# Softmax denominators from added key tiles, and expert tiles in reverse order with fewer waits between scatter-adds, in a hybrid conv, attention and mixture-of-experts layer

## The chip, the cores and the metric

The kernel runs on 1 core of one Trainium2 chip. The metric is the device time of one execution in microseconds (us); the time before is a median of 3 runs. Engines are called TensorE (PE, and PEld for its weight loads), VectorE (DVE), ScalarE (ACT), GpSimd (POOL) and SyncE (SP, which issues DMAs).

## The reference

The input x is 8 batches of 512 channels on 16 x 16 positions, so 256 tokens of 512 channels each. Three residual layers follow each other:

```python
x = x + _L0_conv_ref(_gn(x), cfc_w, bn_w, bn_b)     # a gate per channel from mean, max, std
t = _to_tokens(x)                                   # [8, 256, 512]
t = t + _L1_attn_ref(_ln_t(t), w_q, w_k, w_v, w_o)
t = t + _L1_ffn_ref(_ln_t(t), ...)
```

The attention has 16 heads of 32. Scores go through 30 * tanh(s / 30), a causal mask (the window of 256 covers all keys) and a softmax; heads are joined by w_o. The feed-forward part adds a shared expert (width 512) and a mixture of 8 experts (width 256): each of the 2048 tokens goes to its two best experts, and their outputs are added with normalised weights.

## The kernel before

Everything is fp32; large products are split into high and low parts (three products each). The engines run one instruction stream each and meet at semaphores; the order on each engine is written out by hand, and an engine that waits holds up all that stands behind it on that engine.

**Attention.** One batch is one `step`; TensorE's step interleaves the scores and values of batch b with the projections of b+1 and the gate of b-1. The 16 heads form 4 groups of 4 (c or g from 0 to 3). The keys are 2 tiles of 128. For each pair of heads `probs` holds 2 x 384 columns: 256 queries for the first key tile, and queries 128 to 255 for the second. Scores (`group_scores`, L1486) go to ScalarE (`tanhs` L656, `exps` L663; tanh of group g waits for `pv_done` of group g-2), then GpSimd zeroes what the causal mask forbids (`mask`, L496), then TensorE's `head_values` (L1501) multiplies with v, and once more with a matrix of ones, which gives the softmax denominators on 32 partitions per head. Four heads lie side by side in the array and in the bank. In the ones products the first key tile takes 256 columns and the second 128 per head. VectorE inverts the denominators (`normalise`, L1072, L1075), ScalarE and GpSimd split the result into high and low (`att_high` L668, `att_low` L502). GpSimd also takes the power for the layer norms (`rstd_of`, L487); VectorE's `second_norm` (L1042) waits for it, TensorE's `gate_transposes` (L1456) for the norm. VectorE's `affine` (L1021), the copies of Q and K out of the bank (L1067) and of the gate's partial products (`partial_out`, L1083) come in that order; TensorE's `gate_logits` (L1533) wait for the last.

**Shared expert and routing.** Eight batches of `shared` on TensorE. Meanwhile VectorE works out the routing: how many 128-row tiles each expert gets, the slot of each token (`pair_slots`, L1263 to L1273), the expert of each tile (`tile_experts`, L1277 to L1281), and one-hot matrices (`one_hots`), which TensorE multiplies into token numbers, weights and destination rows of each slot (`place`, L1669; `slots_out`). GpSimd and ScalarE split the expert weights (`weight_low` L548, `weight_high` L741). SP stores each batch's tokens with the shared part to the output, and 128 filler rows behind it.

**Routed experts.** NTILES = 39 tiles of 128 slots, by expert. Per tile: GpSimd gathers 128 token rows (`gather`, L570), TensorE transposes them, multiplies with the expert's weights (L1406), transposes (L1711) and multiplies again (L1720); VectorE scales by the slot's weight into one of three buffers `yo` (`expert_out`, L1377), and GpSimd adds the rows to the output with an accumulating indirect DMA (`scatter_add`, L580). Two tiles of one expert have no token in common; tiles of different experts may. Slots without a token go to the filler rows. Each scatter-add waits until the one before has landed (`y_added`).

## Time and profile before

| what | value |
|---|---|
| median of 3 runs | 744.7 us (744.04 to 745.97) |
| the profiled execution | 744.78 us, span 743.1 us |
| granted TensorE clock, mean | 0.988 |
| PE busy | 646.3 us (87%) |
| PEld busy | 523.6 us (70%) |
| DVE busy | 402.7 us (54%) |
| POOL busy | 277.6 us (37%) |
| ACT busy | 262.0 us (35%) |
| chain that ended last | PE 57%, DMA 26%, DVE 10%, issue 4%, ACT 2%, POOL 1% |
| of it, scatter-adds of `yo` | 25% |

Shares are of the span. Busy times overlap between engines. A matmul's record lasts until its modelled end, and the next begins before that, so the distance between starts tells more than the duration. The chain is followed back from the last instruction, at each step to what released it.

### The profile page before, as it was taken

To read this page: it belongs to the slowest core of one execution; us is meant where nothing else is said; L and a number is where in the kernel's file an instruction comes from. 1 tells how busy PE (TensorE), PEld (TensorE's weight loads), DVE (VectorE), ACT (ScalarE), POOL (GpSimd) and SP (SyncE) were. 2 spreads that over 40 slices of the span, in tenths; PEclk is the share of its full clock that TensorE was granted. 3 is DMA by queue.
4 is the path that set the end of the run, shared out by engine and by line. 5 is a ranking of instruction groups with operands and counts; after the bars stand their busy time and mean duration, and the time that the engine had idled before them with its cause. 6 is when DMAs were issued, how large, how long until landed. Compare 5 with 4: busy or idle time off the path is not lost.

```text
span 743.1 us, 13600 instructions
## 1 busy us (share of the span) xinstructions
PE 646.3 (87%) x4859; PEld 523.6 (70%) x4860; DVE 402.7 (54%) x1021; ACT 262.0 (35%) x463; POOL 277.6 (37%) x324
## 2 busy tenths in 40 slices
PE   0112699999999999999999999999799999999991
PEld 0101688888888888888689899998566767667660
DVE  7886346566666656564556994223444443444430
ACT  7440155454454545364433223435112122121110
POOL 1980022323323222231411115857245445455431
PEclk9999999999999999999999999999999999999996
DMA  9540000010000101020125333442665555655533
GB/s 310 171 142 0 1 1 2 20 40 28 28 28 28 42 15 56 0 76 12 42 100 223 119 104 115 144 149 86 239 112 92 109 98 99 111 95 105 104 55 40
DMA packets 24786, 62.08 MB, mean 84 GB/s; under 512 B 3056, under 2 KB 7152, under 8 KB 23728
## 3 DMA queue, kind: packets, MB, share of 16 engines
q1 hardware_dynamic: 15344, 41.16, 16.1%
q0 software_dynamic: 8736, 20.45, 15.4%
q8 instruction: 20, 0.33, 0.2%
q10 hardware_dynamic: 672, 0.03, 0.1%
q14 instruction: 14, 0.11, 0.0%
HBM read 38.56 MB, written 23.07 MB: 83 GB/s over the span
## 4 chain that ended last, share of the span: by engine, by line
PE 57%; DMA 26%; DVE 10%; issue 4%; ACT 2%; POOL 1%; SPq 0%; DVEq 0%; POOLq 0%
PE PS L1406 25%; DMA out_tokens<-yo,dest 25%; PE scores L1406 13%; PE scores L1639 5%; PE PS L1501 5%; PE scores L1486 4%; PE PS L1456 2%; DVE v L898 2%; PE PS L1445 1%; DMA T<-in_x 1%; ACT probs L656 1%; DVE qT L834 1%; DVE qT L835 1%; PE PS L1524 1%; DVE wgu_l L1351 1%
## 5 line engine op out<-in xcount | busy, mean ns | idle before, releaser
L1406 PE MATMUL scores<-xb,sw 128*128 128x256 f32 x768 | 98.3, 284 | 0.0
L1406 PEld LDWEIGHTS scores<-xb,sw 128*128 128x128 f32 x768 | 95.8, 192 | 2.5 <-issue 0.8
L580 POOL DMA_INDIRECT out_tokens<-yo,dest x39 | 61.7, 1583 | 93.4 <-DMA out_tokens<-yo,dest 91.2
L496 POOL TENSOR_SCALAR_AFFINE_SELECT probs<-probs 128x256 f32<-128x256 f32 x128 | 49.9, 424 | 117.2 <-ACT probs L663 117.1
L1406 PE MATMUL PS<-xt_h,w_h 128*128 128x256 f32 x256 | 75.3, 294 | 1.5 <-DVE xt_l L1057 1.5
L1720 PE MATMUL scores<-wd_sb,ehT 128*128 x156 | 73.5, 593 | 1.0 <-DVE ehT L1366 1.0
L1406 PE MATMUL PS<-xt_l,w_h 128*128 128x256 f32 x256 | 73.0, 285 | 0.0
L1406 PE MATMUL PS<-xt_h,w_l 128*128 128x256 f32 x256 | 72.9, 285 | 0.0
L785 ACT ACTIVATE es<-scores 128x256 f32<-128x256 f32 x39 | 14.9, 383 | 163.3 <-PE scores L1406 163.3
L1406 PE MATMUL scores<-wgu_h,xgT_h 128*128 x156 | 65.4, 419 | 4.3 <-DVE xgT_l L1370 4.3
L1072 DVE RECIPROCAL rden<-PS 128x256 f32<-128x256 f32 x32 | 56.1, 1754 | 17.1 <-PE PS L1501 16.2
L1362 DVE TENSOR_TENSOR eh<-scores,es 128x256 f32<-128x256 f32 x39 | 16.5, 424 | 86.8 <-ACT es L785 86.8
L1406 PE MATMUL scores<-wgu_h,xgT_l 128*128 x156 | 61.7, 395 | 0.0
L1406 PE MATMUL scores<-wgu_l,xgT_h 128*128 x156 | 61.4, 394 | 0.0
L656 ACT ACTIVATE probs<-scores 128x768 f32<-128x768 f32 x64 | 48.4, 810 | 27.0 <-PE scores L1486 27.0
L508 POOL TENSOR_TENSOR hl<-hf,hh 128x256 fp32r<-128x256 f32 x32 | 28.5, 891 | 77.3 <-ACT hh L730 77.3
L502 POOL TENSOR_TENSOR att_l<-att,att_h 128x256 fp32r<-128x256 f32 x32 | 24.0, 751 | 89.0 <-ACT att_h L668 89.0
L1406 PEld LDWEIGHTS PS<-xt_h,w_h 128*128 128x128 f32 x256 | 49.7, 194 | 3.7 <-DVE xt_l L1057 1.8
L663 ACT ACTIVATE probs<-probs 128x768 f32<-128x768 f32 x64 | 50.6, 849 | 0.0
L1406 PEld LDWEIGHTS PS<-xt_l,w_h 128*128 128x128 f32 x256 | 49.8, 195 | 0.0
L1406 PEld LDWEIGHTS PS<-xt_h,w_l 128*128 128x128 f32 x256 | 49.7, 194 | 0.0
L570 POOL DMA_INDIRECT xg<-x_rows,ids x39 | 39.4, 1011 | 21.7 <-PE PS L1663 17.7
(256 smaller groups left out, 1331.7 us busy)
## 6 DMA issues: line engine op xcount, KB each, us to landing
wgu_l<-in_wgu SPq DMA_DIRECT2D x8, 1024.0 KB, 6.8
T<-in_x SPq DMA_DIRECT2D x8, 512.0 KB, 8.2
probs<-in_wqkvo SPq DMA_DIRECT2D x8, 512.0 KB, 3.5
x_rows<-x SPq DMA_DIRECT2D x8, 512.0 KB, 2.8
x_cols<-x2T SPq DMA_DIRECT2D x8, 512.0 KB, 2.8
xc<-x_cols SPq DMA_DIRECT2D x8, 512.0 KB, 3.5
out_tokens<-T SPq DMA_DIRECT2D x8, 512.0 KB, 7.4
wd_sb<-in_wd SPq DMA_DIRECT2D x8, 512.0 KB, 6.7
```

What stands on the lines that cost most here:

```text
L496: ins = pool.affine_select(out=t, in_=t, compare_op=ALU.is_ge, fill=0.0, base=0, pattern=[[0, 2], [1, P]], channel_multiplier=-1)
L508: pool.tensor_tensor(hl[:, j, :], hf[:, j % 2, :], hh[:, j, :].bitcast(fp32), ALU.subtract).then_inc(hl_done, 1)
L570: pool.indirect_dma_start(xg[:, t % 3, :], None, x2_rows[:, :], bass.IndirectOffsetOnAxis(ids[:, t:t + 1], 0)).then_inc(xg_loaded[t % 3], 16)
L580: pool.indirect_dma_start(out[:, :], bass.IndirectOffsetOnAxis(dest[:, t:t + 1], 0), yo[:, t % 3, :], None, compute_op=ALU.add).then_inc(y ...
L656: act.activation(probs[:, p % 4, :].rearrange("p (h q) -> p h q", h=2), scores[:, 2 * (p % 2):2 * (p % 2) + 2, 0:384], ACT.Tanh, scale=1.0 ...
L663: act.activation(probs[:, p % 4, :], probs[:, p % 4, :], ACT.Exp, scale=SOFTCAP).then_inc(exp_done, 1)
L1072: dve.wait_ge(dve_step, step_of(dve.reciprocal(rden[:, :], od_bank[:, S:2 * S])))
L1406: ins = pe.matmul(out, lhs(k, a), rhs(k, b), start=m == 0, stop=m == len(products) - 1)
L1486: ins = pe.matmul(score_bank[j][:, tt * S:S + tt * P], kT[j * D:(j + 1) * D, g, tt * P:(tt + 1) * P], qT[j * D:(j + 1) * D, g, tt * P:S], ...
L1501: ins = pe.matmul(od_bank[j * D:(j + 1) * D, off + tt * P:off + S], lhs(h, tt), pr[:, 0:S] if tt == 0 else pr[:, S:S + P], start=tt == 0, ...
L1639: ins = pe.matmul(dn_bank[tt], (hh, hl)[a][:, j, tt * P:(tt + 1) * P], wslice((sw_h, sw_l)[c], 2, j, 0, C), start=j == 0 and m == 0, stop= ...
L1720: ins = pe.matmul(ey_bank, ehT[:, k * P:(k + 1) * P], w[:, k * C:(k + 1) * C], start=k == 0, stop=k == I // P - 1)
```

## The change

- `head_values`: the ones products take 128 columns each: per head the first half of the queries from `probs`, the second half from `ksum`, the sum of both key tiles' weights. GpSimd makes these sums (`key_sum`, 128 x 512 elements per group of four heads, two buffers) behind the masks of each group; TensorE waits for them ahead of its last four products.
- Tiles are numbered in reverse (`pair_slots`, `tile_experts`), so unused tiles come first. VectorE also works out for each tile the count that its scatter-add waits for (`landed_for`): the landing of the scatter before at the first tile of an expert and at unused tiles, else nothing that is still open. GpSimd reads it into a register for each tile.
- `yo` has two buffers with a semaphore each; VectorE's loop over tiles has two per turn instead of three.
- The filler rows are stored by GpSimd in two halves, instead of by SP.

```diff
...
-        PROBS, SMALL, BATCH = 4 * 2 * 384, 1840, CB * S
+        landed_for = sb("landed_for", [1, NTILES], i32)
+        PROBS, SMALL, BATCH = 4 * 2 * 384, 1856, CB * S
...
+        KEY_SUMS = MAIN - 2 * HC * P
...
+        scope = area("key_sums", KEY_SUMS)
+        ksum = sb("ksum", [P, 2, HC, P], fp32, scope)
+        scope.close()
...
-                if b == 3:
-                    sp.wait_ge(dn_free, 1)
-                    sp.dma_start(out[B * S:B * S + P, :], at(T, 0)[:, 0:C]).then_inc(residual_stored[0], 16)
...
+            def key_sum(b, c, first=False):
+                pool.wait_ge(mask_done, 8 * b + 2 * c + 2)
+                if not (first and c < 2):
+                    pool.wait_ge(pv_done, 4 * b + c - 1)
+                pr = probs[:, 2 * (c % 2):2 * (c % 2) + 2, :].rearrange("p a (h q) -> p (a h) q", h=2)
+                pool.tensor_tensor(ksum[:, c % 2, :, :], pr[:, :, P:2 * P], pr[:, :, 2 * P:3 * P],
+                                   ALU.add).then_inc(ksum_done, 1)
             def att_low(b, c):
...
             def step(b, has_back, has_front, has_next):
                 mask(b, 2)
                 mask(b, 3)
+                key_sum(b, 1, isinstance(b, int) and b == 0)
...
                     rstd_of(var2_ready, rstd2_ready, b - 1)
                 att_low(b, 0)
...
                     rstd_of(var2_ready, rstd2_ready, b - 1)
                 mask(b, 4)
                 mask(b, 5)
+                key_sum(b, 2)
                 att_low(b, 1)
                 mask(b, 6)
                 mask(b, 7)
+                key_sum(b, 3)
                 att_low(b, 2)
                 att_low(b, 3)
...
                     mask(b + 1, 0)
                     mask(b + 1, 1)
+                    key_sum(b + 1, 0)
             rstd_of(var1_ready, rstd1_ready, 0)
             mask(0, 0)
             mask(0, 1)
+            key_sum(0, 0, True)
             rstd_of(var1_ready, rstd1_ready, 1)
             step(0, False, True, True)
             with pool.Fori(1, B - 2) as b:
...
-            def scatter_add(t):
+            def landing_count(t):
+                return pool.value_load(landed_for[0:1, t:t + 1], min_val=16, max_val=16 + 16 * (NTILES // YO + 1))
+            def scatter_add(t, landed):
...
-                        pool.wait_ge(residual_stored[b], 16 if b else 32)
+                        pool.wait_ge(residual_stored[b], 16)
+                    for k in range(YO):
+                        pool.wait_ge(y_landed[k], 16)
...
-                    pool.wait_ge(y_added, 16 * t)
+                    pool.wait_ge(y_landed[(t - 1) % YO], landed)
+                    stand_alone(pool)
...
-                pool.indirect_dma_start(out[:, :], bass.IndirectOffsetOnAxis(dest[:, t:t + 1], 0), yo[:, t % 3, :],
-                                        None, compute_op=ALU.add).then_inc(y_added, 16)
+                pool.indirect_dma_start(out[:, :], bass.IndirectOffsetOnAxis(dest[:, t:t + 1], 0), yo[:, t % YO, :],
+                                        None, compute_op=ALU.add).then_inc(y_landed[t % YO], 16)
+                return landing_count(t + 1) if t + 1 < NTILES else None
+            pool.wait_ge(dn_free, 1)
+            for k in range(YO):
+                pool.dma_start(out[B * S + 64 * k:B * S + 64 * (k + 1), :],
+                               at(T, 0)[64 * k:64 * (k + 1), 0:C]).then_inc(y_landed[k], 16)
             low_with_weights(4, (0, 1, 2, 3))
             low_with_weights(5, (4, 5, 6, 7))
...
+            pool.wait_ge(firsts_ready, 1)
             low_with_weights(6, (), (0, 1, 2))
             low_with_weights(7, (8, 9, 10))
             weight_low(13)
+            landed = None
             for t in range(3, NTILES):
                 gather(t)
...
-                    scatter_add(t - 5)
+                    landed = scatter_add(t - 5, landed)
             for t in range(NTILES - 5, NTILES):
-                scatter_add(t)
-            pool.wait_ge(y_added, 16 * NTILES)
+                landed = scatter_add(t, landed)
+            for k in range(YO):
+                pool.wait_ge(y_landed[k], 16 + 16 * len(range(k, NTILES, YO)))
...
                     if b == 5 and j == 0:
-                        act.wait_ge(residual_stored[0], 32)
+                        for k in range(YO):
+                            act.wait_ge(y_landed[k], 16)
+                        act.wait_ge(residual_stored[0], 16)
...
                     if b == 5 and j == 2:
...
+                dve.wait_ge(dve_step, step_of(dve.tensor_scalar(slot_f[:, 1, :], slot_f[:, 1, :], -1.0,
+                                                                float(NTILES - 1), ALU.mult, ALU.add)))
             def tile_experts():
-                dve.wait_ge(dve_step, step_of(dve.tensor_tensor(
-                    te[:, :, :], iota_f[0:1, 0:NTILES].unsqueeze(2).to_broadcast([1, NTILES, E]),
-                    s8[0:1, 2, :].unsqueeze(1).to_broadcast([1, NTILES, E]), ALU.is_ge)))
-                dve.wait_ge(dve_step, step_of(dve.tensor_reduce(te_f[:, :], te[:, :, :], AX.X, ALU.add)))
-                dve.tensor_scalar(tile_expert[:, :], te_f[:, :], -1.0, None, ALU.add).then_inc(experts_ready, 1)
+                step_of(dve.tensor_tensor(ends[:, 1, :], s8[0:1, 2, :], s8[0:1, 1, :], ALU.add))
+                dve.wait_ge(dve_step, n.value())
+                dve.wait_ge(dve_step, step_of(dve.tensor_scalar(ends[:, 0, :], ends[:, 1, :], -1.0, float(NTILES),
+                                                                ALU.mult, ALU.add)))
+                turn = iota_f[0:1, 0:NTILES]
+                for t, op in ((te, ALU.is_ge), (te_is, ALU.is_equal)):
+                    step_of(dve.tensor_tensor(t[:, :, :], turn.unsqueeze(2).to_broadcast([1, NTILES, E]),
+                                              ends[:, 0, :].unsqueeze(1).to_broadcast([1, NTILES, E]), op))
+                dve.wait_ge(dve_step, n.value())
+                step_of(dve.tensor_reduce(te_f[:, :], te[:, :, :], AX.X, ALU.add))
+                step_of(dve.tensor_reduce(strict[:, 0, :], te_is[:, :, :], AX.X, ALU.max))
+                dve.wait_ge(dve_step, n.value())
+                dve.wait_ge(dve_step, step_of(dve.tensor_scalar(strict[:, 1, :], te_f[:, :], -1.0, float(E), ALU.mult,
+                                                                ALU.add)))
+                dve.tensor_scalar(tile_expert[:, :], strict[:, 1, :], float(E - 1), None,
+                                  ALU.min).then_inc(experts_ready, 1)
+                step_of(dve.tensor_scalar(strict[:, 2, :], te_f[:, :], 0.0, None, ALU.is_equal))
+                dve.wait_ge(dve_step, n.value())
+                step_of(dve.tensor_tensor(strict[:, 3, :], strict[:, 0, :], strict[:, 2, :], ALU.max))
+                step_of(dve.tensor_scalar(strict_i[:, 0, :], turn, 8.0, 8.0, ALU.mult, ALU.add))
+                dve.wait_ge(dve_step, n.value())
+                dve.wait_ge(dve_step, step_of(dve.tensor_scalar(strict_i[:, 1, :], strict_i[:, 0, :], 4, 4,
+                                                                ALU.logical_shift_right, ALU.logical_shift_left)))
+                dve.wait_ge(dve_step, step_of(dve.tensor_copy(strict[:, 0, :], strict_i[:, 1, :])))
+                dve.wait_ge(dve_step, step_of(dve.tensor_tensor(strict[:, 1, :], strict[:, 0, :], strict[:, 3, :],
+                                                                ALU.mult)))
+                dve.tensor_scalar(landed_for[:, :], strict[:, 1, :], 16.0, None, ALU.add).then_inc(firsts_ready, 1)
             def one_hots(g):
...
                 dve.wait_ge(ey_full, t + 1)
...
-                    dve.wait_ge(y_added, 16 * (t - 2))
+                    dve.wait_ge(y_landed[k], 16 + 16 * uses)
...
-            def three_tiles(i, start=False, end=False):
-                for k in range(3):
-                    hidden(3 * i + k)
-                    if not (end and k == 2):
-                        x_low(3 * i + k + 1)
-                    if k == 0 and not start:
-                        expert_out(3 * i - 1, 2, i - 1)
-                    elif k:
-                        expert_out(3 * i + k - 1, k - 1, i)
-                    hidden_T(3 * i + k)
+            def tile_steps(t, odd, pair, start=False, end=False):
+                hidden(t)
+                if not end:
+                    x_low(t + 1)
+                if not start:
+                    expert_out(t - 1, 1 - odd, pair if odd else pair - 1)
+                hidden_T(t)
...
-            three_tiles(0, start=True)
-            three_tiles(1)
-            with dve.Fori(2, NTILES // 3 - 1) as i:
-                three_tiles(i)
-            three_tiles(NTILES // 3 - 1, end=True)
-            expert_out(NTILES - 1, 2, NTILES // 3 - 1)
+            for t in range(3):
+                tile_steps(t, t % 2, t // 2, start=t == 0)
+            with dve.Fori(1, (NTILES - 1) // 2 - 1) as i:
+                tile_steps(2 * i + 1, 1, i)
+                tile_steps(2 * i + 2, 0, i + 1)
+            tile_steps(NTILES - 2, 1, (NTILES - 2) // 2)
+            tile_steps(NTILES - 1, 0, (NTILES - 1) // 2, end=True)
+            expert_out(NTILES - 1, 0, (NTILES - 1) // 2)
...
                 pe.wait_ge(mask_done, 8 * b + 2 * c + 2)
...
                     pe.wait_ge(att_ready, 4 * b + c)
-                for off, lhs in ((0, lambda h, tt: v[:, tt, h * D:(h + 1) * D]), (S, lambda h, tt: ones[:, 0:D])):
-                    for tt in range(TT):
-                        for j in range(HC):
-                            h = HC * c + j
-                            pr = probs[:, (h // 2) % 4, 384 * (h % 2):384 * (h % 2 + 1)]
-                            ins = pe.matmul(od_bank[j * D:(j + 1) * D, off + tt * P:off + S], lhs(h, tt),
-                                            pr[:, 0:S] if tt == 0 else pr[:, S:S + P], start=tt == 0, stop=tt == TT - 1,
-                                            skip_group_check=True)
+                def weights(j):
+                    h = HC * c + j
+                    return h, probs[:, (h // 2) % 4, 384 * (h % 2):384 * (h % 2 + 1)]
+                for tt in range(TT):
+                    for j in range(HC):
+                        h, pr = weights(j)
+                        pe.matmul(od_bank[j * D:(j + 1) * D, tt * P:S], v[:, tt, h * D:(h + 1) * D],
+                                  pr[:, 0:S] if tt == 0 else pr[:, S:S + P], start=tt == 0, stop=tt == TT - 1,
+                                  skip_group_check=True)
+                for j in range(HC):
+                    pe.matmul(od_bank[j * D:(j + 1) * D, S:S + P], ones[:, 0:D], weights(j)[1][:, 0:P], start=True,
+                              stop=True, skip_group_check=True)
+                pe.wait_ge(ksum_done, 4 * b + c + 1)
+                for j in range(HC):
+                    ins = pe.matmul(od_bank[j * D:(j + 1) * D, S + P:2 * S], ones[:, 0:D], ksum[:, c % 2, j, :],
+                                    start=True, stop=True, skip_group_check=True)
...
             def out_projection(part, b, s, item="OP"):
```

## Rows read from the trace of the kernel before

**Rows 1.** stages: us; busy PE, PEld, DVE, ACT, POOL (count); clock, DMA share, GB/s

```profile
110.00:340.00 230.00, 228.64 (x2390) 193.07 (x2391) 144.19 (x271) 112.17 (x178) 67.72 (x143) 1.00 0.08 30
...
535.00:743.00 208.00, 191.71 (x817) 132.59 (x814) 82.43 (x150) 35.66 (x73) 94.38 (x72) 0.97 0.53 92
```

**Rows 2.** who waited for whom in the routed experts, total, times, longest

```profile
POOL out_tokens L580 <- DMA out_tokens<-yo,dest: 88.0, 37, 3.7
...
DVE yo L1377 <- PE scores L1720: 23.5, 38, 2.2
```

**Rows 3.** VectorE in order of time, tiles 5 and 38: start, duration, engine, line

```profile
560.96 0.75 DVE L1377 TENSOR_SCALAR yo<-scores,slot_w 128x512 f32<-128x512 f32 x1 [0.63 <-PE scores L1720]
...
727.79 0.75 DVE L1377 TENSOR_SCALAR yo<-scores,slot_w 128x512 f32<-128x512 f32 x1 [2.16 <-PE scores L1720]
```

**Rows 4.** GpSimd in order of time, tile 5

```profile
562.51 1.59 POOL L580 DMA_INDIRECT out_tokens<-yo,dest  x1 [2.29 <-DMA out_tokens<-yo,dest]
```

**Rows 5.** end of the chain that ended last: start, duration, what

```profile
731.36 1.55 POOL out_tokens L580
```

**Rows 6.** TensorE in order of time, batch 4: the ones block and its waits

```profile
249.42 0.83 PE L1501 MATMUL PS<-probs,ones 128*32 128x256 f32 x16
...
255.82 0.94 PE L1486 MATMUL scores<-qT,kT 32*128 32x256 f32 x16 [0.20 <-ACT probs L656]
256.68 1.09 PE L1456 MATMUL PS<-ident,x 128*128 128x128 f32 x8
...
262.44 0.61 PE L1533 MATMUL PS<-fold,rden 128*128 128x8 f32 x4
```

**Rows 7.** TensorE, what is in flight at 249.90: from the second ones wave on

```profile
249.63 0.51 PE L1501 MATMUL PS<-probs,ones 128*32 128x256 f32 x8
```

**Rows 8.** GpSimd additions and subtractions, two sizes: count, busy us, mean ns

```profile
L502 POOL TENSOR_TENSOR att_l<-att,att_h 128x256 fp32r<-128x256 f32 x32 | 24.0, 751 | 89.0 <-ACT att_h L668 89.0
...
L482 POOL TENSOR_TENSOR w_l<-probs,w_h 128x1024 fp32r<-128x1024 f32 x8 | 18.7, 2387 | 15.3 <-ACT w_h L623 15.3
```

**Rows 9.** GpSimd and VectorE in the same batch

```profile
253.22 0.69 POOL L487 TENSOR_TENSOR rstd<-var_eps,powers 128x2 f32<-128x2 f32 x1 [0.43 <-DVE var_eps L1037]
...
254.02 1.33 DVE L1042 TENSOR_SCALAR x<-T,mean_var,rstd 128x512 f32 x2
...
255.69 1.76 DVE L1072 RECIPROCAL rden<-PS 128x256 f32<-128x256 f32 x1 [0.34 <-PE PS L1501]
...
256.66 1.49 POOL L496 TENSOR_SCALAR_AFFINE_SELECT probs<-probs 128x256 f32<-128x256 f32 x4 [2.05 <-ACT probs L663]
...
257.82 1.91 DVE L1021 TENSOR_SCALAR front<-T,coefA,coefB 128x256 f32 x4
...
260.68 0.69 DVE L1067 COPY kT<-PS 128x512 f32<-128x512 f32 x1 [0.94 <-PE PS L1406]
...
261.40 0.42 DVE L1083 COPY rden<-PS 128x256 f32<-128x256 f32 x1
```

**Rows 10.** affine map of batch 4, last three operations: duration ns min, median, max

```profile
L1021 DVE TENSOR_SCALAR front<-T,coefA,coefB x3: 402/405/869, 258.2 to 258.9; 128x256 f32 x3
```

**Rows 11.** TensorE at the first one-hot products

```profile
414.88 0.66 PE L1669 MATMUL PS<-oh_tile,oh_row 128*128 128x120 f32 x4 [0.81 <-DVE oh_tile L1295]
```

**Rows 12.** VectorE and GpSimd around the experts of the tiles

```profile
448.48 0.46 DVE L1277 TENSOR_TENSOR te<-iota_f,s 1x312 f32<-1x312 f32 x1
...
450.29 0.24 DVE L1306 TENSOR_SCALAR unused<-slot_w,spare_row 128x39 f32<-128x39 f32 x1
...
452.32 0.42 DVE L1123 TENSOR_TENSOR hf<-scores,sg 128x256 f32<-128x256 f32 x1 [1.45 <-ACT sg L728]
...
453.27 0.74 POOL L508 TENSOR_TENSOR hl<-hf,hh 128x256 fp32r<-128x256 f32 x1 [3.45 <-ACT hh L730]
453.31 1.29 DVE L1197 TENSOR_TENSOR T<-scores,T 128x512 f32<-128x512 f32 x2 [0.56 <-PE scores L1639]
```

**Rows 13.** TensorE in the same stretch

```profile
455.96 0.63 PE L1639 MATMUL scores<-sw,hh 128*128 128x512 f32 x2
```

15 lines of the change are left out of this document (10 added, 5 removed).

## The prediction

> **What bounds the kernel now.** I read the table by stages first [rows 1]. In the attention batches (110 to 340 us) TensorE is busy 228.64 of 230 us, in the routed experts (535 to 743, with the tail) 191.71 of 208: TensorE is the wall, and an edit elsewhere pays only if it lets TensorE run sooner.
>
> The chain that ended last says otherwise for the last stage: it runs through the landings of the scatter-adds. So I looked at who waits there [rows 2]. GpSimd waits 88.0 us in 37 pieces for a scatter to land, but VectorE, which writes `yo`, waited for nothing but TensorE (23.5 us in 38 pieces); had the scatters set the pace, it would have waited for a buffer. The distance from the end of a `yo` to its scatter says the same. Tile 5: yo starts at 560.96 and lasts 0.75, ending at 561.71 [rows 3]; its scatter starts at 562.51 [rows 4], 0.80 later. Of the 39 tiles none has a shorter distance, and many have this one, so the scatter chain just keeps up. Only at the end, where TensorE has no next tile and the last yo comes early, does it fall behind: tile 38's yo ends at 727.79 + 0.75 = 728.54 [rows 3], its scatter starts at 731.36 [rows 5], 2.82 later. So the chain of scatters owns only 2.82 - 0.80 = 2.0 us of the span.
>
> **Part 1, the scatter-adds.** With the wait only at a change of expert, tile 38's scatter (a tile of the same expert went before it, unless that expert has one tile only) can start 0.80 us after its yo: -2.0 us, all of it on the path. The cost of the register load and the register wait per tile on GpSimd doesn't show in the trace of before; its bounds are 0 and the longest thing GpSimd issues here, 1.59 us [rows 4]. It stands after a scatter, where GpSimd idles 88.0 / 37 = 2.4 us per tile [rows 2], so I take 0; if that cover were gone, only the last tile would feel it. Two buffers instead of three: yo of tile t now waits for the scatter of t-2, which before landed ahead of the scatter of t-1, since that one waited for it; yo of t comes still later. I take 0, and no gain in the middle of the stage, where TensorE sets the pace. Order of the experts: all weights are waited for at the start anyway, 0.
>
> **Part 2, fewer columns on TensorE.** Four heads run side by side, one record each, so a wave of four is the unit. In the ones block the 256-column wave lasts from 249.42 [rows 6] to 249.63 [rows 7]: 0.21 us; a 128-column wave is half. Before: two of 256 and two of 128. After: four of 128. Saved 2 x 0.105 = 0.21 us per group of four heads, 32 groups: 6.8 us at most.
>
> Where does it arrive? Per batch there are four groups. Group 1's saving is lost: scores of group 3 already wait for ScalarE's tanh (0.20 idle at 255.82 [rows 6]), and the tanh hangs on the scores before group 1, not on group 1. Groups 0, 2 and 3 have TensorE work right behind: 3 x 0.21 = 0.63 per batch.
>
> **Part 3, the new wait and GpSimd's sums.** An addition of 128x512 is not in the trace. Bounds: 0.75 us (128x256) and 2.39 (128x1024) [rows 8]; between them linearly 1.3 us, which I take, and 0.2 as allowance for its two waits. Group 1 is tightest. Its masks end at 253.22 - 0.43 = 252.79 [rows 9], so the sum is there at 254.3. TensorE asks for it before the last two waves of the block. The old block let the next work start at 255.82 - 0.20 = 255.62 [rows 6]; the new one does so 0.21 sooner, and 0.21 sooner again because of group 0; two waves (0.21) and 0.2 as allowance for their drain before that is 254.8: 0.5 us to spare. The wait itself I count at 0 while it is satisfied: in the old block TensorE runs wave after wave, and the new one leaves that as it is. The other groups have more room.
>
> Behind the sum, in GpSimd's order, stands rstd2 (253.22 before [rows 9], now 254.3, +1.07), and behind that, on VectorE, the second norm (254.02, ending 255.35). It now ends at about 256.4; TensorE's gate transposes, at 256.68 [rows 6] less 0.21, come just behind: no stall, with no margin either. VectorE's reciprocal, at 255.69, had 0.34 idle ahead of it [rows 9], so its later work moves by 1.07 - 0.34 = 0.73: the affine map from 257.82 to 258.55. There it meets the next new sum, which runs from 256.66 + 1.49 - 0.21 [rows 9] + 0.2 to 259.4. A GpSimd addition holds up such a VectorE operation: of three affine operations two take 402 and 405 ns and one, beside GpSimd's subtraction of 0.75 [rows 8], 869 [rows 10]. So the first of the four is held by some 0.65, and the affine map, K's copy and the copy of the gate partials end 0.73 + 0.65 - 0.94 = 0.44 later (0.94 was idle before K's copy at 260.68 [rows 9]), at 261.40 + 0.42 + 0.44 = 262.26. TensorE's gate logits wait for that copy; they stood at 262.44 [rows 6] and without it would now start at 262.02. So of 0.42 gained by then 0.2 stays, and with group 3 the batch gains 0.4 instead of 0.63. That holds for batches 1 to 5; batch 0 has no gate logits and 6 no affine map.
>
> The Trainium skill, "SBUF — State Buffer", section "SBUF: two separate sides", has GpSimd and VectorE share one port pair that the first to start holds for its whole instruction. The trace agrees for VectorE's side [rows 10], and the sum above is made with it; without any such hold it would be 0.23 x 5 = 1.1 us better, 738.1.
>
> The last batch has other work between its groups; I count 0.2 for each of its groups 0, 2 and 3 there too.
>
> Attention: 0.63 + 5 x 0.4 + 0.63 + 0.6 = 3.9 us. Bounds: 6.8 with nothing given back; below nothing if the sum is long (rival A).
>
> **Part 4, routing on VectorE.** One more dependent operation in `pair_slots`. TensorE idles 0.81 us for the first one-hots [rows 11], so that chain is the path: +0.24, by the nearest small operation [rows 12]. In `tile_experts` there come one more 312-element comparison and its reduction (0.46 each, [rows 12]) and ten small ones at 0.24 or less, about 3.1 us. Before hf of batch 4 at 452.32 VectorE idled 1.45, so add_shared(3) moves by 1.65 from 453.31 to about 455.0 and ends, 1.29 long, at 456.2 [rows 12], where TensorE starts the next down product at 455.96 [rows 13]. I take 0.1, since small operations that don't wait for each other overlap; bounds 0 (more overlap) and 1.2 (0.1 more for each). Together +0.3.
>
> **Part 5, the filler rows.** Their store leaves SP's queue for two stores of GpSimd's, in front of `low_with_weights(4)`. SP loses one short issue. GpSimd idles 3.45 us there, ahead of `hl` at 453.27 [rows 12]; two issues at 1.59 at most [rows 4] are 3.2, so the cover holds; without it `hl` and TensorE's down product would be late by what is over.
>
> **Sum.** -2.0 - 3.9 + 0.3 = -5.6 us. The profiled execution took 744.78 (span 743.1), within 0.1 of the median 744.7, so no correction: 739.1 us.
>
> **Rivals.** About 0.3% (2.2 us) is what a measurement here tells from no change; below 742.5 is faster.
>
> A, slower: the sums are longer than I take. Mechanism: a long sum of group 1 pushes rstd2, the second norm and so TensorE's gate transposes, and group 2's sum pushes the affine map and the gate logits. At 2.39 us [rows 8] the second norm ends at 257.5 and the transposes lose 0.8 against before; the logits come at 263.6, 1.2 late, less 0.2 from group 3: +1.0 x 5, batch 6 +0.4, the last +0.7, batch 0 -0.6: +5.5 instead of -3.9, so 748.5. Linear in between, the whole turns slower than before from about 1.9 us on. Against it: two rows enclose the size, and the masks, strided in the same way, are short. 7%.
>
> B, all of part 2 arrives (6.8), because VectorE isn't held or group 1 counts too: -2.0 - 6.8 + 0.3, 736.2. For it: TensorE is busy throughout [rows 1]. 17%.
>
> C, nothing of part 2 arrives: each gain is waited off at tanh, second norm or logits, which run behind TensorE by tenths only. 744.7 - 2.0 + 0.3 = 743.0, no change. 15%.
>
> D, the tail isn't freed (the wait holds in every tile, or two scatters in flight land later by as much): 744.7 - 3.9 + 0.3 = 741.1. Against it: the last tiles belong to one expert. 11%.
>
> **How the numbers follow.** Forecast 739.1, 50%. The range reaches from just below B to just above C, 735.6 to 743.3; A and the outer parts of B and C are left out, about 2 in 10. Faster: forecast, B, D and the better edge of C, 0.78; within 0.3%: most of C, 0.15; slower: A, 0.07.
>
> **What would show it.** In the profile after: ones matmuls of 128 columns only; GpSimd's new additions at 1.3 us (over 1.9: A); scores of group 3 still waiting for ScalarE; a short wait of the gate logits for the copy of the partials in batches 1 to 5 and a batch period some 0.4 us shorter; the yo period unchanged, GpSimd no longer waiting for landings in most tiles, and the last scatter 0.8 us after the last yo instead of 2.82. A period of yo that shrinks would prove wrong that TensorE paces the experts; a TensorE wait for the sums of group 1, that they are short enough.

## The result, and the profile after

| | before | after |
|---|---|---|
| device time, median of the runs | 744.78 us (744.04 to 745.97, 4 runs) | 735.15 us (734.28 to 735.54, 4 runs) |
| span of the profiled execution | 743.1 us | 733.0 us |

The ratio is 0.9869 (95% interval 0.9853 to 0.9885): faster by 9.6 us, where 5.6 were forecast. Measured beside before on another chip, the changed kernel gave 735.14 and 0.9872 (0.9857 to 0.9887).

I cut both spans at the same work and compare the pieces; the landmarks are rows in order of time.

| from ... to | before, us | after, us | difference | forecast |
|---|---|---|---|---|
| start ... reciprocal of batch 0, group 0 | 106.97 | 106.38 | -0.59 | 0 |
| ... of batch 7, group 0 | 245.19 | 241.14 | -4.05 | -3.3 |
| ... last reciprocal (batch 7, group 3) | 18.76 | 17.17 | -1.59 | -0.6 |
| ... first one-hot product | 43.96 | 44.12 | +0.16 | +0.2 |
| ... first yo | 120.18 | 121.03 | +0.85 | +0.1 |
| ... last yo | 192.73 | 192.99 | +0.26 | 0 |
| ... start of the last scatter-add | 3.57 | 1.21 | -2.36 | -2.0 |
| ... end of the span | 11.69 | 8.99 | -2.70 | 0 |

The pieces add up to -10.0. The first is no effect of the change: two executions of the changed kernel take 106.38 and 108.19 us there. Now the rows behind the others. In the routed experts GpSimd, which waited 88.0 us for landings [rows 2], now waits mostly for `yo`, and VectorE's `yo` still for nothing but TensorE (waits of the stretch: total, times, longest):

```profile
POOL out_tokens L616 <- DVE yo L1452: 53.0, 29, 3.6
...
POOL out_tokens L616 <- DMA out_tokens<-yo,dest: 25.2, 9, 4.1
...
DVE yo L1452 <- PE scores L1805: 22.9, 39, 2.2
```

A tile in the middle and the last one, in order of time (start, duration, engine, line), to be held against [rows 3 to 5]:

```profile
555.65 0.75 DVE L1452 TENSOR_SCALAR yo<-scores,slot_w 128x512 f32<-128x512 f32 x1 [0.50 <-PE scores L1805]
...
556.86 1.59 POOL L616 DMA_INDIRECT out_tokens<-yo,dest  x1 [0.30 <-issue]
...
722.83 0.75 DVE L1452 TENSOR_SCALAR yo<-scores,slot_w 128x512 f32<-128x512 f32 x1 [2.16 <-PE scores L1805]
...
724.04 1.55 POOL L616 DMA_INDIRECT out_tokens<-yo,dest  x1 [1.87 <-DVE yo L1452]
```

The last scatter starts 724.04 - 723.58 = 0.46 us after the last `yo` ends, where it was 2.82.

The new sums as a group (count, busy us, mean ns, idle before), and the matmuls that read them:

```profile
L516 POOL TENSOR_TENSOR ksum<-probs 128x512 f32<-128x512 f32 x32 | 41.3, 1291 | 3.5 <-POOL probs L504 1.7
...
L1587 PE MATMUL PS<-ksum,ones 128*32 128x128 f32 x256 | 12.9, 273 | 0.4 <-POOL ksum L516 0.4
```

1.29 us each, and TensorE waited 0.4 us for them in the whole kernel, in one piece in the last batch (who waited for whom, 340 to 405 us):

```profile
PE PS L1587 <- POOL ksum L516: 0.4, 1, 0.4
```

Batch 4 in order of time, against [rows 6, 9]; first GpSimd and VectorE, then TensorE:

```profile
247.77 1.74 DVE L1118 RECIPROCAL rden<-PS 128x256 f32<-128x256 f32 x1
...
250.14 1.27 POOL L516 TENSOR_TENSOR ksum<-probs 128x512 f32<-128x512 f32 x1 [0.17 <-POOL probs L504]
...
250.16 1.28 DVE L1083 TENSOR_SCALAR var_eps<-mean_var 128x2 f32<-128x2 f32 x1
...
251.51 0.71 POOL L495 TENSOR_TENSOR rstd<-var_eps,powers 128x2 f32<-128x2 f32 x1
...
252.34 1.32 DVE L1088 TENSOR_SCALAR x<-T,mean_var,rstd 128x512 f32 x2 [0.31 <-POOL rstd L495]
...
255.22 1.30 POOL L516 TENSOR_TENSOR ksum<-probs 128x512 f32<-128x512 f32 x1
...
255.69 2.38 DVE L1067 TENSOR_SCALAR front<-T,coefA,coefB 128x256 f32 x4
...
258.59 0.41 DVE L1129 COPY rden<-PS 128x256 f32<-128x256 f32 x1
...
283.44 1.74 DVE L1118 RECIPROCAL rden<-PS 128x256 f32<-128x256 f32 x1
```

```profile
251.99 0.40 PE L1587 MATMUL PS<-ksum,ones 128*32 128x128 f32 x8
...
252.80 0.94 PE L1561 MATMUL scores<-qT,kT 32*128 32x256 f32 x16 [0.41 <-ACT probs L700]
...
253.71 1.09 PE L1531 MATMUL PS<-ident,x 128*128 128x128 f32 x8
...
259.25 0.61 PE L1618 MATMUL PS<-fold,rden 128*128 128x8 f32 x4
```

Three things are to be seen here. Scores of group 3 wait 0.41 for tanh (0.20 before). The transposes follow `x` (252.34 + 1.32 = 253.66) at once. The gate logits (259.25) come 0.25 after the copy of the partials (259.00) and wait for nothing that counts. The reciprocals of group 0 in two batches that follow each other give the batch period, 35.67 us. Before, it was 36.26, and the variance, which now lasts 1.28 us beside the sum, lasted 0.17:

```profile
250.57 1.74 DVE L1072 RECIPROCAL rden<-PS 128x256 f32<-128x256 f32 x1
...
252.96 0.17 DVE L1037 TENSOR_SCALAR var_eps<-mean_var 128x2 f32<-128x2 f32 x1
...
286.83 1.74 DVE L1072 RECIPROCAL rden<-PS 128x256 f32<-128x256 f32 x1
```

Two pieces of the table are TensorE's clock. In before the stretch 362.8 to 366.2 us, in the last batch, ran at a granted clock of 0.50 (1.2 GHz); I call this a half-clock stretch. After has none there, and at the first expert tiles one of 6.8 us, where before has one of 3.4 (from 523.2). Columns as in [rows 1]; first before, then after:

```profile
362.80:366.20 3.40, 3.40 (x37) 2.55 (x28) 1.69 (x2) 2.75 (x4) 2.15 (x5) 0.50 0.41 154
```

```profile
515.60:522.40 6.80, 5.11 (x12) 4.07 (x13) 2.58 (x4) 0.00 (x0) 0.48 (x1) 0.50 1.00 346
```

### The profile page after: what moved, and what is told of

It is laid out like the page before. It is cut to its first block, busy times and chain, and to the rows that moved or that the text cites. A ratio compares the mean times of both kernels' runs of the same rounds, so it can differ in the third digit from the quotient of the medians.

```text
span 733.0 us, 13855 instructions
## 1 busy us (share of the span) xinstructions
PE 639.1 (87%) x4859; PEld 521.9 (71%) x4860; DVE 414.8 (57%) x1034; ACT 262.7 (36%) x463; POOL 319.9 (44%) x358
## 4 chain that ended last, share of the span: by engine, by line
PE 83%; DVE 10%; issue 2%; ACT 2%; DMA 1%; POOL 1%; SPq 0%; DVEq 0%; POOLq 0%
PE scores L1481 27%; PE PS L1481 25%; PE scores L1805 9%; PE scores L1724 5%; PE scores L1561 4%; PE PS L1578 2%; PE PS L1748 2%; PE PS L1531 2%; DVE v L944 2%; PE PS L1520 1%; PE PS L1796 1%; DMA T<-in_x 1%; ACT probs L700 1%; DVE qT L880 1%; DVE qT L881 1%
## 5 line engine op out<-in xcount | busy, mean ns | idle before, releaser
L831 ACT ACTIVATE es<-scores 128x256 f32<-128x256 f32 x39 | 14.9, 383 | 164.4 <-PE scores L1481 164.4
```

## The experiments

Unless said otherwise, ratios are against the kernel before, run beside it on the same chip.

**The two halves apart.** One kernel has only the key sums, the other everything else.

```diff
+                    pe.matmul(od_bank[j * D:(j + 1) * D, S:S + P], ones[:, 0:D], weights(j)[1][:, 0:P], start=True,
...
+                pe.wait_ge(ksum_done, 4 * b + c + 1)
...
```

> The kernel before with the denominators from key sums alone; experts, routing and scatter-adds as before. Theory S (the gain is two separate gains): attention as in the changed kernel, about -0.6 per batch for batches 0 to 6 (-4.2), and -1.2 more if the half-clock stretch of the last batch (3.4 us at 362.8 in the kernel before) stays away; tail as before (last scatter 2.8 us after the last yo, GpSimd's closing drain 6.4 us): 744.8 - 4.2 to 5.9 = 738.9 to 740.6. Theory P (my prediction's attention term, the rest of the gain comes from the scatters): -3.9, 740.9, and a half-clock stretch at the last batch as before. Rival K (the drain at the end is shorter for another reason than the scatters): drain near 3.75 us here too, and 736.2 to 737.9.

Measured: 740.76 us, ratio 0.9948 (0.9934 to 0.9963): -3.9 us by the ratio, -3.2 by the medians. The time alone does not tell theory S from theory P; the landmarks below do.

```diff
-                    pool.wait_ge(y_added, 16 * t)
+                    pool.wait_ge(y_landed[(t - 1) % YO], landed)
...
```

> The kernel before with everything but the key sums: experts in reverse, waits only at a change of expert, two yo buffers, filler rows stored by GpSimd. Theory S: attention batches as before with the half-clock stretch at 362.8; +0.2 in the one-hots; last scatter 0.5 to 0.8 us after the last yo (-2.0 to -2.4) and the closing drain 3.75 instead of 6.4 us (-2.7): 744.8 + 0.2 - 4.7 to 5.1 = 739.9 to 740.3, and up to 0.9 more or less with the clock at the experts' start. Theory P (my prediction's tail: the drain as before): 744.8 - 2.0 + 0.3 = 743.1. Rival K: drain 6.4 us here.

Measured: 740.26 us, 0.9948 (0.9932 to 0.9964): -3.9 us by the ratio, -3.7 by the medians. Landmarks: with the key sums alone, batches 0 to 6 take 241.16 us (-4.03, as in after), the last batch 18.66, with the half-clock stretch; from the last scatter to the end 11.4 us. With the rest alone, batches 0 to 6 take 245.18, the last scatter starts 0.46 after the last `yo`, and from there to the end it is 8.9. So attention belongs to the sums, tail and end to the scatter part. The kernel with the sums alone has tiles 5.148 us apart instead of 5.121, 1.0 us in all, for which I found no cause. The two ratios together make 7.8 of the 9.6 us; these slower tiles and the half-clock stretch of the first kernel's profiled execution are about what is missing, but no run shows that they are it.

The second kernel also prices the clock. Its last batch has the old denominators, as before, and no half-clock stretch. Reciprocals of groups 0 and 3 in batch 7, before and then this kernel:

```profile
352.16 1.75 DVE L1072 RECIPROCAL rden<-PS 128x256 f32<-128x256 f32 x1
...
370.92 1.76 DVE L1072 RECIPROCAL rden<-PS 128x256 f32<-128x256 f32 x1 [3.84 <-PE PS L1501]
```

```profile
352.68 1.75 DVE L1096 RECIPROCAL rden<-PS 128x256 f32<-128x256 f32 x1
...
369.87 1.76 DVE L1096 RECIPROCAL rden<-PS 128x256 f32<-128x256 f32 x1 [3.17 <-PE PS L1554]
```

18.76 against 17.19 us: 1.57 for the same instructions. After has 17.17, so the new denominators gained 0.02 us in the last batch, and the other 1.57 of its -1.59 are the clock.

**A landing wait in every tile.**

```diff
-                step_of(dve.tensor_scalar(strict[:, 2, :], te_f[:, :], 0.0, None, ALU.is_equal))
+                step_of(dve.tensor_scalar(strict[:, 2, :], te_f[:, :], 0.0, None, ALU.is_ge))
```

> The changed kernel, but every tile's scatter waits for the landing of the one before it (the flag that says where an expert begins is true for every tile; register load and two buffers stay). Theory S, drain tied to the chain of landings: last scatter 2.8 us after the last yo and drain 6.4 us: 735.2 + 2.3 + 2.7 = 740.2. Theory T, the lag comes back but the drain is set by something else of the change (two buffers, two semaphores, who stores the filler rows): 735.2 + 2.3 = 737.5 with a drain of 3.75 us. Theory U, two buffers with the chain now pace VectorE too: yo waits for landings and the tiles' period grows from 5.13 us towards the chain's own, 743 or more.

Measured: 755.59 us, 1.0151 (1.0118 to 1.0185), 20 us above the changed kernel; theory U, and more than the 743 that it named as the least. Waits in the experts, then two scatter-adds in order of time:

```profile
POOL out_tokens L616 <- DMA out_tokens<-yo,dest: 105.5, 37, 4.0
...
DVE yo L1452 <- DMA out_tokens<-yo,dest: 83.4, 28, 4.4
```

```profile
643.53 1.59 POOL L616 DMA_INDIRECT out_tokens<-yo,dest  x1 [2.85 <-DMA out_tokens<-yo,dest]
...
649.12 1.59 POOL L616 DMA_INDIRECT out_tokens<-yo,dest  x1 [2.72 <-DMA out_tokens<-yo,dest]
```

They are 5.59 us apart. A landing comes 4.8 us after its scatter starts, here as in before, so 0.8 us pass from a landing to the next scatter; in before, at 5.13 us a tile, some 0.3 did. The wait against a register, with the semaphore increment that follows it, thus costs about half a microsecond where landings are waited for, and then the landings pace VectorE through the two buffers. In most tiles the changed kernel does not wait there, and so keeps the tiles' old distance. The end (from the last scatter) is 9.0 us here too: the short end does not come from freeing the chain.

**Every key sum twice.**

```diff
+                pool.tensor_tensor(ksum[:, c % 2, :, :], pr[:, :, P:2 * P], pr[:, :, 2 * P:3 * P],
+                                   ALU.add).then_inc(ksum_once, 1)
+                pool.wait_ge(ksum_once, 4 * b + c + 1)
```

> The changed kernel, but every key sum is made twice, one after the other, so that a sum is ready 2.6 us after its masks instead of 1.3. Rival A's price in my prediction: at 2.39 us the attention costs +5.5 instead of -3.9, a difference of 9.4 us, and at 2.6 us some 11: 735.2 + 11 = about 746, slower than the kernel before; TensorE waits at the gate transposes (second norm late) and at the gate logits. Rival L (there is more room than I worked out, as the gate logits of the changed kernel did not wait at all): TensorE waits only for the sums of group 1, some 0.8 us per batch, and 735.2 + 6 = 741. Rival N: no wait, 735.2 within 0.5.

Measured: 750.01 us, 1.0074 (1.0052 to 1.0096), 14.9 above the changed kernel and slower than before. TensorE's waits from 110 to 340 us:

```profile
PE PS L1535 <- DVE x L1092: 5.4, 6, 0.9
PE PS L1591 <- POOL ksum L520: 4.4, 7, 0.7
...
PE PS L1622 <- DVE rden L1133: 0.8, 3, 0.3
```

Rival A's mechanism is real: 0.9 us per batch at the gate transposes, where I had worked out 0.8 for 2.39 us, and little at the logits. The wait for the sum itself, 0.7, was not in its price. An ordinary batch takes 37.29 us instead of 35.66; the idle TensorE then fell to 1.2 GHz for 3.4 us at 150.0, 300.1 and 375.2 us, and the two batches from group 0 to group 0 with the first two of these took 1.2 us more than the others.

**Where the end's 2.7 us come from.** No instruction of the change stands behind the last landing. The trace records there the drain with which GpSimd's instructions end: 6.44 us in before, 3.75 in after. First one kernel with SP's store put back, and one with GpSimd's stores alone:

```diff
-            for k in range(YO):
-                pool.dma_start(out[B * S + 64 * k:B * S + 64 * (k + 1), :],
-                               at(T, 0)[64 * k:64 * (k + 1), 0:C]).then_inc(y_landed[k], 16)
+                    sp.dma_start(out[B * S:B * S + P, :], at(T, 0)[:, 0:C]).then_inc(residual_stored[0], 16)
```

> The changed kernel with one thing undone: the filler rows are stored by SP in one piece, as in the kernel before, not by GpSimd in two. It asks where the 2.7 us at the very end come from (GpSimd's closing drain lasts 6.44 us in the kernel before and 3.75 in the changed one, and 3.75 with a landing wait in every tile too). Theory F (the drain's length goes by what GpSimd's own DMA queue has carried): drain 6.44 again, 735.2 + 2.7 = 737.9. Theory G (it goes by the semaphores or the buffers of the scatter-adds, one before, two now): drain 3.75 and 735.2.

```diff
-                    sp.dma_start(out[B * S:B * S + P, :], at(T, 0)[:, 0:C]).then_inc(residual_stored[0], 16)
+            for k in range(2):
+                pool.dma_start(out[B * S + 64 * k:B * S + 64 * (k + 1), :],
+                               at(T, 0)[64 * k:64 * (k + 1), 0:C]).then_inc(filler_stored, 16)
```

> The kernel before with one thing changed: the filler rows are stored by GpSimd in two pieces instead of by SP in one; scatter chain, three buffers, order of experts and denominators as before. Theory F: GpSimd's closing drain is 3.75 us instead of 6.44, and the time is 744 - 2.7 = 741.3, though no work of the path has changed. Theory G: drain 6.44 and no change against the kernel before.

Measured: 738.11 us, 0.9925 (0.9901 to 0.9949), drain 6.44; and 744.82 us, 1.0013 (1.0003 to 1.0023), drain 6.52. The first fits theory F, the second breaks it. A difference that is left between the second and the changed kernel is the semaphore on which GpSimd's plain stores count. So once more before, with the stores on the scatters' semaphore (shown against the run just told; the waits on it then count the two stores too), and after, with them on one of their own:

```diff
-                               at(T, 0)[64 * k:64 * (k + 1), 0:C]).then_inc(filler_stored, 16)
+                               at(T, 0)[64 * k:64 * (k + 1), 0:C]).then_inc(y_added, 16)
```

```diff
-                               at(T, 0)[64 * k:64 * (k + 1), 0:C]).then_inc(y_landed[k], 16)
+                               at(T, 0)[64 * k:64 * (k + 1), 0:C]).then_inc(filler_stored, 16)
```

> The kernel before, with the filler rows stored by GpSimd in two pieces whose landings are counted on the same semaphore as the scatter-adds'. (With a semaphore of their own the closing drain stayed at 6.5 us.) Theory V (the drain is short where a plain store of GpSimd's shares the scatters' semaphore): drain 3.75. Theory W (it takes the two buffers and two semaphores of the changed kernel as well): drain 6.4 to 6.5.

> The changed kernel, with the filler rows stored by GpSimd as there, but counted on a semaphore of their own, so that the two semaphores of the scatter-adds count scatter-adds alone. Theory V (the shared semaphore makes the drain short): drain 6.4 to 6.5 and about 738. Theory W (two buffers and GpSimd's stores make it short, whatever the semaphore): drain 3.75 and 735.2.

Measured, one execution each: 741.67 us with a drain of 3.75, and 738.22 with 6.52. The last scatter of the one, then of the other:

```profile
731.17 1.55 POOL L577 DMA_INDIRECT out_tokens<-yo,dest  x1 [3.57 <-DMA out_tokens<-yo,dest]
```

```profile
724.68 1.55 POOL L616 DMA_INDIRECT out_tokens<-yo,dest  x1 [1.88 <-DVE yo L1451]
```

The spans are 740.0 and 736.4 us: 8.8 and 11.7 us from the last scatter to the end. Theory V: the end is short where the filler stores of GpSimd count on the scatters' own semaphores, whatever the rest of the kernel is. All 17 traces agree: 3.75 us in the 12 with that sharing, 6.44 or 6.52 in the 5 without. Why the drain goes by that stays open; that these semaphores are then the first that GpSimd's queue uses was not told apart from the sharing.

**Can group 1's saving be had?** It is the 0.41 us at tanh. First: scores of group 2 earlier, by cutting Q's projection; `between` runs ahead of the last four products.

```diff
-                heads_projection(part, "Q0", b)
-                group_scores(b, 2)
+                heads_projection(part, "Q0", b, lambda: group_scores(b, 2))
```

> The changed kernel, with scores of group 2 four products earlier on TensorE (the last four products of Q's first half projection come behind them), so that ScalarE's tanh of group 2 starts some 0.45 us sooner. In the changed kernel scores of group 3 wait 0.41 us per batch for it, which is where the saving of group 1 went. Theory H (that wait takes the place of the gain, and the second norm on VectorE, whose end the gate transposes follow by 0.05 us, is the next): the wait for tanh goes, a wait of the gate transposes for x of 0.3 to 0.4 comes, and the time stays within 0.5 us of 735.2. Rival I (nothing stands behind it): -0.41 x 6 or 7 = -2.5 to -2.9 us, 732.5.

Measured: 735.63 us, 0.9889 (0.9872 to 0.9905): theory H. The wait moved to `x` (TensorE, 110 to 340 us):

```profile
PE PS L1533 <- DVE x L1088: 2.5, 6, 0.5
```

Next, the second norm's variance and rstd2 earlier as well:

```diff
+                if has_back:
+                    variance(var2_ready)
                 normalise(b, 0, first)
-                if has_back:
-                    variance(var2_ready)
...
+                if has_back and has_front:
+                    rstd_of(var2_ready, rstd2_ready, b - 1)
                 mask(b, 2)
                 mask(b, 3)
                 key_sum(b, 1, isinstance(b, int) and b == 0)
-                if has_back and has_front:
-                    rstd_of(var2_ready, rstd2_ready, b - 1)
```

> As the run with scores of group 2 earlier, and the second norm's variance (VectorE) and rstd2 (GpSimd) moved ahead of group 0's normalisation and of group 1's masks, so that they no longer run beside or behind the key sum of group 1 (the variance lasts 1.28 us there, held by the sum). Theory H: x of the second norm is ready about a microsecond sooner, no wait of the gate transposes, and 0.41 x 6 = -2.5 us against the changed kernel: 732.7. Rival J (GpSimd's masks of group 1, 0.7 later by rstd2, or VectorE's group 0, 0.9 later, now stand ahead of TensorE): TensorE waits at group 1, and 735.2 to 738.

Measured: 733.50 us, 0.9861 (0.9845 to 0.9878). That is between theory H and rival J. TensorE waits for nothing in the batches, but the batch period is 35.57 us, only 0.1 less than in the changed kernel: cutting the projection itself costs 0.20 (its 24 products and the scores take 4.13 us instead of 3.93). The profiled span is 2.2 us shorter than in the run before: batches 0 to 6 make 1.6 of it (240.25 for 241.83), and the first expert tiles 0.9, where this execution has a half-clock stretch of 3.4 us and that one has 6.8.

Then with the projection whole again (`second_norm` also goes ahead of `project_out(part, "Q0", b)`):

```diff
-                group_scores(b, 3)
                 if has_back:
                     gate_transposes(part, b - 1, b)
+                group_scores(b, 3)
                 heads_projection(part, "K0", b)
```

> The changed kernel with the second norm early (variance on VectorE and rstd2 on GpSimd ahead of group 0's normalisation and group 1's masks, x ahead of Q's copy) and the gate transposes on TensorE ahead of scores of group 3 instead of behind them, so that they fill the 0.41 us in which these scores wait for tanh; Q's projection stays in one piece. Theory H (group 1's saving is there to be had, and the run with Q's projection cut in two gave back part of it at the two extra changes between kinds of products): no wait for tanh, none for x, batch period 35.66 - 0.41 = 35.25, and 735.2 - 6 x 0.41 = 732.7. Rival K (TensorE's own stream is the bound and the 0.41 turns up elsewhere, as 0.33 of it did with Q's projection cut): batch period about 35.6 and 734.5 to 735.2.

Measured: 735.42 us, 0.9880 (0.9864 to 0.9897): rival K. In the middle batches no wait for tanh is left, but rstd2 now holds up group 1's masks, and the block of the key sum starts 0.27 us late and the transposes take 0.17 more.

And with the statistics earlier, in `add_attention`:

```diff
                                       ALU.add).then_inc(ring_free[k], 1)
+                    if tt == 0 and part in ("first", "mid"):
+                        dve.wait_ge(*emptied(part, f"{item}0", s))
+                        stand_alone(dve)
+                        step_of(dve.bn_stats(bn6[:, 0, :], tile_at(b, 0)))
```

> As the run with the second norm early and the gate transposes ahead of scores of group 3, and VectorE's statistics of the first half of the rows directly behind that half's addition, in its idle 2 us, so that variance and rstd2 end 0.65 us sooner and group 1's masks and key sum are no longer pushed back by rstd2 (there the saved 0.41 had gone: 0.27 to the key sum of group 1, 0.17 to x). Theory H: no wait of TensorE for tanh, key sum or x in the batches, batch period 35.66 - 0.41 = 35.25, and 735.2 - 2.5 = 732.7. Rival K: the wait moves on again, batch period 35.6 and 734.5 to 735.2.

Measured: 733.81 us, 0.9856 (0.9841 to 0.9872), beside 735.14 for the changed kernel. Reciprocals of group 0 in batches 4 and 5:

```profile
248.51 1.76 DVE L1118 RECIPROCAL rden<-PS 128x256 f32<-128x256 f32 x1
...
283.86 1.76 DVE L1118 RECIPROCAL rden<-PS 128x256 f32<-128x256 f32 x1
```

A period of 35.35 us, 0.31 of the 0.41; the time lies between theory H and rival K. So most of the saving was there, behind three waits a few tenths deep: tanh, the second norm, the key sum.

**The ends of the stages.** The last batch's edit (with ScalarE's tanh and exp of group 2, and GpSimd's masks, moved ahead to match) and the first tile's:

```diff
-                out_projection(part, b - 1, b, "OQ")
-                group_scores(b, 2)
+                out_projection(part, b - 1, b, "OQ", lambda: group_scores(b, 2))
```

```diff
             x_low(0)
+            for m in DVE_SPLITS[2:]:
+                weight_low(m)
             add_shared(B - 1)
...
-            pe.wait_ge(wgu_l_dve, len(DVE_SPLITS))
+            pe.wait_ge(wgu_l_dve, 2)
...
+                    if start and k == 1:
+                        pe.wait_ge(wgu_l_dve, len(DVE_SPLITS))
```

> As the run with the second norm early and the gate transposes ahead of scores of group 3, and two more stalls of the changed kernel filled. In the last batch, scores of group 2 stand between the two halves of the output projection of the batch before and their tanh no longer waits for its end (there TensorE idles 0.41 + 1.59 + 0.40 us). At the first expert tile VectorE splits the tile's rows ahead of the last two weight blocks, which belong to the expert that comes last (there TensorE idles 3.75 us for that split), and TensorE waits for these blocks one tile later. Expected: -2.5 from the batches, -1.5 in the last batch, -2.2 at the first tile: 735.2 - 6.2 = 729.0. If the stalls only move on: 732.7 as in the run without these two edits.

Measured: 734.95 us, 0.9867 (0.9851 to 0.9884). The first tile's edit worked (TensorE's wait there 1.5 us, not 3.7); the last batch's did not: TensorE waits 2.9 us in one piece for `att` of group 1. VectorE makes it behind the statistics and the variance of the second norm, and its reciprocal starts only at 359.30, though GpSimd had freed the buffer by 358.37. The half-clock stretch is back too. So the next has the early statistics and the first tile's edit alone:

> As the run before it, and VectorE splits the first expert tile's rows ahead of the last two weight blocks (expert 0, which comes last in the reverse order), with TensorE's wait for these blocks one tile later. By the earlier run that had this edit, TensorE's idle time at the first tile falls from 3.75 to 1.5 us. Theory H: 732.7 - 2.2 = 730.5. Rival K: 735.2 - 2.2 = 733.

Measured: 732.46 us (731.27 to 733.87, 5 runs), 0.9840 (0.9827 to 0.9854): by the median the fastest version here, 2.7 us below the changed kernel beside it, but nearer to rival K's 733 than to theory H's 730.5. Its trace shows no half-clock stretch before the tail.

The last experiment is the changed kernel itself, without an edit.

> The changed kernel once more, beside the two others of this call. It tells whether the half-clock stretches stay where they were (3.4 us lost at the last batch in some executions of some kernels, none here so far; 3.4 or 6.8 us at the first expert tiles): if they belong to the kernel they stand at the same work again, if they belong to the execution they move. 735.2, closing drain 3.75 us.

Measured: 735.14 us (734.50 to 736.36). At the first expert tiles its trace has a half-clock stretch of 3.4 us where the first profile of the same kernel has one of 6.8, and takes 120.24 us from the first one-hot to the first `yo` instead of 121.03. Of the kernels with before's last batch, two have the stretch there and two (among them the one with a drain of 6.52) do not, though TensorE idles 1.57 to 1.58 us in one piece ahead of that place in all four. So these stretches move with the execution; each is worth 0.8 to 1.6 us, and neither sign of it is an effect of the change.

## Why the prediction was wrong in size, step by step

The time fell 0.45 us outside the range. The direction and the two mechanisms (fewer columns on TensorE, the tail freed) were right.

- **What lay behind the last scatter.** The step that failed: "the chain of scatters owns only 2.82 - 0.80 = 2.0 us of the span". I took everything from the last scatter to the end as fixed. It shortened by 2.70 us, through a store that Part 5 counted at nothing. Without it after would have stood at 735.15 + 2.7 = 737.9, inside the range; the kernel with SP's store shows 738.11, the one with the stores on a semaphore of their own 738.22.
- **Tail.** -2.36 for -2.0. The 0.80 us from `yo` to scatter was no floor: it was what the chain left, and the free distance is 0.28 to 0.46.
- **Batches 0 to 6.** -4.05 for -3.3, or 0.60 per middle batch for 0.40. The term that was mis-sized: the copy of the gate partials was to end "0.73 + 0.65 - 0.94 = 0.44 later", so that 0.2 would come back at the logits. The copy ended 0.25 ahead of them and nothing came back. Counted from the start of group 0's reciprocal it ends no later than before (11.23 us, 11.25 before). The affine map started 0.67 later, not 0.73, and grew by 0.47 (2.38 for 1.91), not by the 0.65 for which the prediction shows no working. The last 0.2 lies in the two copies: their records now overlap the operation ahead (257.99 against 258.07, 258.59 against 258.67), where before they started behind it. Groups 0, 2 and 3 gave their 0.21 each, less 0.05 at the transposes; group 1 gave none, as forecast.
- **Sum and margins.** 1.29 us for 1.3. Group 1's sum ended at 251.41, 0.58 before the matmuls that read it at 251.99 (forecast 0.5). The transposes follow `x` by 0.05, the "no margin either". One link I had not seen: the variance, 0.17 us in before, lasts 1.28 beside the sum. It started at 250.16, 0.02 behind the sum, and ended at 251.44, 0.03 behind the sum's end. The Trainium skill, "SBUF — State Buffer", section "SBUF: two separate sides", says that the loser of the pair that the two engines share waits for the whole instruction; this row agrees, with 1.28 beside an addition of 1.27. GpSimd's masks show no such hold: the affine operations beside them take up to 0.50 us, 0.40 alone.
- **Last batch.** Forecast -0.6, measured -0.02 besides the clock. TensorE's waits there grew by what the three blocks saved, 0.63: for tanh 0.41 us instead of 0.20, and 0.40 that is new, for the sum of group 2; the 1.6 us for masks stayed. Part 3 had said that the groups other than 1 have more room, and I had spread the rule of the middle batches over the last without looking for its waits.
- **Routing and tiles.** +0.16 for +0.24; `tile_experts` cost nothing that shows: with a half-clock stretch of 3.4 us, as before has it, the changed kernel takes 120.24 us to the first `yo`, 0.06 more than before. The 38 tiles take 0.26 us longer, about the 0 taken for the two buffers; whether it is these was not told apart.
- **Clock.** -1.57 and about +0.8 in the two profiled executions, not forecast, by accident of the executions. How much of it the medians hold is not known.
- **Rivals.** D (tail not freed) was priced at 741.1; with the wait in every tile the kernel takes 755.6, since I had counted the register wait at 0 on the ground that GpSimd idles anyway. That cover is gone as soon as landings are waited for. A is real, with its wait for the sum left out. B, 736.2, was nearest to the time, but not for its reasons: group 1 did not count, and VectorE was held. C, that nothing of part 2 arrives, is out with the 4.05 of batches 0 to 6.
- **Sums.** Four figures of the prediction are off by a little, none of which changes the 739.1: 32 x 0.21 is 6.7, not 6.8; 739.1 - 1.1 is 738.0, not 738.1; two operations at 0.46 and ten at 0.24 are 3.3, not about 3.1; and 0.50 + 0.17 + 0.11 is 0.78 without any edge of C.

## What to carry to other kernels

A span ends behind the last useful instruction: compare what lies there in both kernels before taking it as fixed. A saving on the busiest engine arrives only where that engine has other work ready behind it; look for the wait that is already there, and for those a few tenths behind it (here there were three). A distance that repeats in every tile can be the pace of a chain rather than the cost of a step.

## What the runs showed of the hardware that I had not expected

- GpSimd's closing drain lasts 3.75 us when its plain stores count on the semaphores of its scatter-adds and 6.44 to 6.52 otherwise; in the kernel before with these stores on GpSimd, the time from the last scatter to the end is 8.8 us with that sharing and 11.6 without.
- A 128x2 operation of VectorE took 1.28 us instead of 0.17 beside a GpSimd addition, yet beside GpSimd's masks (1.49 us for four) operations of VectorE that take 0.40 us alone took no more than 0.50.
- The same work of TensorE runs at 2.4 GHz in one execution and for 3.4 us at 1.2 GHz in the next, 1.57 us apart in the last batch, behind the same idle time.
